# Attention tiles: 512-wide score reductions, transpose copies shared by ScalarE and VectorE, a second P buffer

## The chip, the cores and the metric

One Trainium2 chip, 8 NeuronCores. Each core runs the same program on its own batch element, with no exchange between cores. The metric is the device time in microseconds of the slowest core.

## The reference

Two layers, each an attention whose output is multiplied by a gate made by a feed-forward network, and added to x. Only the attentions matter here:

```python
# layer 0: 16 heads of 128, causal, own K and V per head
scores = jnp.einsum('bhqd,bhkd->bhqk', q, k) * scale
scores = jnp.where(causal, scores, jnp.finfo(scores.dtype).min)
probs = jax.nn.softmax(scores, axis=-1)
attn = jnp.einsum('bhqk,bhkd->bhqd', probs, v)
# layer 1: 16 query heads, one K and one V for all, no mask
scores = jnp.einsum('bhqd,bkd->bhqk', q, k) * SCALE
attn = jax.nn.softmax(scores, axis=-1)
out = jnp.einsum('bhqk,bkd->bhqd', attn, v)
# both layers
x = x + s * g
```

The sequence has 2048 positions, so a head has 16 query tiles of 128 rows.

## The kernel before

The program is a row of phases, each ended on all engines before the next starts: layer norm, QKV, attention, output projection, feed-forward, for each layer, and a final sum. The attention phase (`phase_att`) runs once per layer, with `L` 0 or 1.

A phase is written as one function per engine: `tenf` (TensorE), `vecf` (VectorE), `scaf` (ScalarE), `syncf` (the DMA queue of SyncE). Each engine goes through its own instructions in the written order; nothing is reordered. They meet at semaphores: `bump` gives a point of one engine's work a name, `wt` makes an engine wait for that point. VectorE and ScalarE are moreover fenced (`_Fence`, line 86): each of their instructions waits until the one before on the same engine is complete, so all of them show line 86 in the profile, with small gaps between them.

The loops run over 16 heads `h` and 16 query tiles `qt`. A tile has `nch` score chunks of 512 keys: always 4 in layer 1; in layer 0 1, 2, 3, 4 for tiles 0-3, 4-7, 8-11, 12-15. The first `ha` chunks lie in the PSUM tensor `SCA`, the other `hb` in `SCB`: 1+0, 1+1, 2+1 or 2+2. A tile goes so:

- TensorE multiplies Q and K into `SCA` (L627) once ScalarE's exponential of the last tile has read it, then into `SCB` (L637) likewise.
- VectorE adds the causal mask to the last chunk (layer 0), takes the negated row maximum of `SCA`, then of `SCB` (`TENSOR_REDUCE`), and their minimum, `negm`.
- ScalarE waits for `negm` and for the transposes of the tile before, and writes exp(score + negm) to `PSB` in 16 bits, the row sums to `za` and `zb`: one `ACTIVATE` for `SCA`, one for `SCB`.
- VectorE waits for the last exponential, adds the sums, takes the reciprocal and scales `PSB` in place (mark `pn`).
- TensorE, which has first issued the scores of the tile after, transposes `PSB` in 128x128 blocks (`transp`, L598) into the two halves of the PSUM tensor `PP`, 8 blocks each. Over 8 blocks (three or four chunks) both halves are used.
- ScalarE copies each half to the SBUF tensor `PT` (`ptevac`), after the exponentials of the tile after.

Every four tiles (a group), TensorE multiplies V with `PT` into `OT` (`_att_pv`, L747, 4 to 16 matmuls), once all of the group's copies are done; VectorE copies `OT` out (`CAST P<-OT`). In program order this stands behind the first tile of the next group (tiles 4, 8, 12), and at a head's end behind tile 15. In the text a group boundary is such a tile 4, 8 or 12.

Names in the profile: `P` is the big SBUF tensor, which holds `PSB`, `PT`, Q, K, V and the attention's output; `st` the small statistics tensor.

Of the kernel before, what the change touches and what calls it, by code (L numbers as in the profile page):

```python
# [13 lines left out]
AX = mybir.AxisListType.X  # L14
# [79 lines left out]
class KB:  # L94
# [471 lines left out]
    def phase_att(self, L):  # L566
# [1 line left out]
        causal = (L == 0)  # L568
        QH = [k.Cp[:, 0:2048], k.Cp[:, 2048:4096]]
        VH = [k.Cp[:, 4096:6144], k.Cp[:, 6144:8192]]  # L570
        PSB = k.Cp[:, 8192:10240]
        PT = k.Cp[:, 10240:18432]
        negma = k.st1[:, 0:1]; negmb = k.st1[:, 1:2]; negm = k.st1[:, 2:3]
        za = k.st1[:, 3:4]; zb = k.st1[:, 4:5]; zs = k.st1[:, 5:6]; rz = k.st1[:, 6:7]

        def nchf(qt):
            return qt // 4 + 1 if causal else 4
# [5 lines left out]
        with self.nc.psum_tensor(f"SCA{L}", [128, 1024], F32) as SCA, \  # L583
# [31 lines left out]
            def tenf(t):  # L615
# [3 lines left out]
                for h in range(HEADS):  # L619
                    k.wt(t, f"a{L}qv_{h}")  # L620
                    for qt in range(NT):
                        ha, hb = haf(qt)
                        kbase = h * 2048 if L == 0 else 0
                        if lastA is not None:
                            k.wt(t, lastA)
                        for c in range(ha):
                            ins = t.matmul(SCA[:, c * 512:(c + 1) * 512],  # L627
                                           QH[h % 2][:, qt * 128:(qt + 1) * 128],
                                           k.Bp[:, kbase + c * 512: kbase + c * 512 + 512],
                                           start=True, stop=True)  # L630
                        k.bump(ins, "sT", mark=f"a{L}scA_{h}_{qt}")
                        lastA = f"a{L}expA_{h}_{qt}"
                        if hb:
                            if lastB is not None:
                                k.wt(t, lastB)
                            for c in range(ha, ha + hb):
                                ins = t.matmul(SCB[:, (c - ha) * 512:(c - ha + 1) * 512],  # L637
                                               QH[h % 2][:, qt * 128:(qt + 1) * 128],
                                               k.Bp[:, kbase + c * 512: kbase + c * 512 + 512],
                                               start=True, stop=True)  # L640
                            k.bump(ins, "sT", mark=f"a{L}scB_{h}_{qt}")
                            lastB = f"a{L}expB_{h}_{qt}"
                        if qt > 0:
                            transp(t, h, qt - 1, ppq)
                            if (qt - 1) % 4 == 3:
                                self._att_pv(t, L, h, (qt - 1) // 4, causal, VH, PT, OT)
                    transp(t, h, NT - 1, ppq)
                    self._att_pv(t, L, h, 3, causal, VH, PT, OT)

            def vecf(v):  # L650
                for h in range(HEADS):
                    for qt in range(NT):
                        nch = nchf(qt)
                        ha, hb = haf(qt)
                        off = qt % 4
                        k.wt(v, f"a{L}scA_{h}_{qt}")
                        if causal and hb == 0:
                            v.tensor_tensor(SCA[:, (ha - 1) * 512:ha * 512],
                                            SCA[:, (ha - 1) * 512:ha * 512],
                                            k.msk()[:, off * 512:(off + 1) * 512], OP.add)  # L660
                        ins = v.tensor_reduce(negma, SCA[:, 0:ha * 512], AX, OP.max, negate=True)
                        k.bump(ins, "sV", mark=f"a{L}negA_{h}_{qt}")
                        if hb:
                            k.wt(v, f"a{L}scB_{h}_{qt}")
                            if causal:
                                v.tensor_tensor(SCB[:, (hb - 1) * 512:hb * 512],
                                                SCB[:, (hb - 1) * 512:hb * 512],
                                                k.msk()[:, off * 512:(off + 1) * 512], OP.add)
                            ins = v.tensor_reduce(negmb, SCB[:, 0:hb * 512], AX, OP.max, negate=True)
                            k.bump(ins, "sV", mark=f"a{L}negB_{h}_{qt}")  # L670
                            k.wt(v, f"a{L}negB_{h}_{qt}")
                            ins = v.tensor_tensor(negm, negma, negmb, OP.min)
                        else:
                            k.wt(v, f"a{L}negA_{h}_{qt}")
                            ins = v.tensor_copy(negm, negma)
                        k.bump(ins, "sV", mark=f"a{L}neg_{h}_{qt}")
# [23 lines left out]
            def ptevac(sc, h, qt):  # L700
                nkb = nchf(qt) * 4
                if qt % 4 == 0:
                    if qt > 0:
                        k.wt(sc, f"a{L}pv_{h}_{qt//4 - 1}")
                    elif h > 0:
                        k.wt(sc, f"a{L}pv_{h-1}_3")
                for b in range((nkb + 7) // 8):
                    k.wt(sc, f"a{L}tpb_{h}_{qt}_{b}")
                    j0, j1 = b * 8, min(nkb, b * 8 + 8)
                    dst = PT.rearrange("p (n t) -> p n t", n=16)[:, j0:j1,  # L710
                                                                 (qt % 4) * 128:(qt % 4) * 128 + 128]
                    src = pph[b % 2][:, 0:(j1 - j0) * 128].rearrange("p (n t) -> p n t", n=j1 - j0)
                    ins = sc.copy(dst, src)
                    k.bump(ins, "sS", mark=f"a{L}pte_{h}_{qt}_{b}")
                k.marks[f"a{L}ptall_{h}_{qt}"] = k.marks[f"a{L}pte_{h}_{qt}_{(nkb-1)//8}"]

            def scaf(sc):
                for h in range(HEADS):
                    for qt in range(NT):
                        ha, hb = haf(qt)  # L720
                        k.wt(sc, f"a{L}neg_{h}_{qt}")
                        if qt > 0:
                            k.wt(sc, f"a{L}tp_{h}_{qt-1}")
                        elif h > 0:
                            k.wt(sc, f"a{L}tp_{h-1}_{NT-1}")
                        ins = sc.activation(PSB[:, 0:ha * 512], SCA[:, 0:ha * 512], AF.Exp,
                                            bias=negm, scale=1.0, accum_out=za)
                        k.bump(ins, "sS", mark=f"a{L}expA_{h}_{qt}")
# [610 lines left out]
```

How the kernel before makes its waits and increments, by code:

```python
    def then_inc(self, *a, **kw):  # L52
        return self
# [27 lines left out]
        def f(*args, **kw):  # L81
            kb = self._kb
            sn = self._sname
            kb.sem(sn)
            self._eng.wait_ge(kb.sem_h[sn], kb.cnt.get(sn, 0))
            ins = real(*args, **kw)
            kb.cnt[sn] = kb.cnt.get(sn, 0) + 1
            if not isinstance(ins, _MockIns):
                ins.then_inc(kb.sem_h[sn], 1)
            return ins
# [20 lines left out]
    def bump(self, ins, n, amt=1, mark=None):  # L111
        if n in AUTOMAP:
            sn = AUTOMAP[n]
            self.sem(sn)
            v = self.cnt.get(sn, 0)
            if mark is not None:
                self.marks[mark] = (sn, v)
            return v
        self.sem(n)
        self.cnt[n] += amt
        if mark is not None:
            self.marks[mark] = (n, self.cnt[n])
        if ins is not None and not isinstance(ins, _MockIns):
            ins.then_inc(self.sem_h[n], amt)
        return self.cnt[n]
# [1 line left out]
    def wt(self, eng, mark):  # L127
        got = self.marks.get(mark)
        if got is None:
            if self.mock:
                return
            raise KeyError(f"unresolved mark {mark}")
        n, v = got
        eng.wait_ge(self.sem(n), v)
# [1 line left out]
    def wtv(self, eng, n, v):  # L136
        eng.wait_ge(self.sem(n), v)
# [166 lines left out]
            def syncf(sy):  # L304
# [14 lines left out]
                    if L == 1:  # L319
                        k.wt(sy, f"ln{L}x1_{i}")
                        sy.dma_start(out=k.x1_h[i], in_=XF[i % 2][:]).then_inc(k.sem("st"), 16)
                        k.bump(None, "st", 16)
```

## Time and profile before

| | us |
|---|---|
| runs of the kernel | 12421.89 and 12107.16, median 12264.52 |
| the profiled execution | 12111.88 |
| its span on the slowest core (5) | 12110.3 |
| spans of the 8 cores | 12086.5 to 12110.3 |
| busy: TensorE, VectorE, ScalarE | 7344.6, 3957.8, 2841.2 |
| attention of layer 0, of layer 1 (first score matmul to the next stage's first rows) | 2042, 2425 |

The profile is of one execution. Its views used below are the busy time of each engine in a stretch, the timeline (each instruction with its start, its length, how long its engine was idle before it and who released it), and groups of like instructions with their mean length. PE is TensorE, PEld its weight loads, DVE VectorE, ACT ScalarE. The granted clock is a share of 2.4 GHz.

### The profile page before, as it was taken

What the parts mean: (1) busy time and instruction counts of PE and PEld (TensorE: products, weight loads), DVE (VectorE), ACT (ScalarE), POOL (GpSimd) and SP (SyncE); (2) the same over time, 40 slices, a digit from 0 to 9 for tenths busy, and PEclk for the clock granted to TensorE, in tenths of its full rate; (3) what the DMA queues carried; (4) which work ended last, traced back from release to release, by engine and by line L of the source; (5) the groups of instructions that cost most, each with busy time, mean ns of one, the idle gap of its engine ahead of it and who ended that gap; (6) DMA issues with size and microseconds to landing.
All of it is one profiled execution on the core that took longest, in us unless ns stands there. A gap on an engine that the chain in (4) does not pass through costs nothing. (4 is left out here: it accounts for less than half of the span.)

```text
span 12110.3 us, 107998 instructions; the slowest of 8 cores (12086.5 to 12110.3 us)
## 1 busy us (share of the span) xinstructions
PE 7344.6 (61%) x35408; PEld 3415.2 (28%) x35408; DVE 3957.8 (33%) x6488; ACT 2841.2 (23%) x4586; POOL 134.9 (1%) x233
## 2 busy tenths in 40 slices
PE   1299444444379999183650855555554799997791
PEld 0144211111134444031220322222222344443340
DVE  4421344444314444815312244444443111110002
ACT  2200333333301111212112044444444000000000
POOL 0000000000000000000000000000000000000000
PEclk9999655555689999596775955555555899998995
DMA  1233000000132331132233300000000322223444
GB/s 47 51 61 56 21 11 7 11 7 11 28 89 48 61 61 37 40 70 49 55 99 130 73 8 8 7 8 7 8 8 13 85 47 53 53 53 81 108 79 168
DMA packets 426199, 581.07 MB, mean 48 GB/s; under 512 B 257200, under 2 KB 347312, under 8 KB 401456
## 3 DMA queue, kind: packets, MB, share of 16 engines
q0 software_dynamic: 75216, 237.39, 11.9%
q1 hardware_dynamic: 350432, 336.77, 8.9%
q8 instruction: 293, 4.80, 0.2%
q14 instruction: 258, 2.11, 0.1%
HBM read 655.71 MB, written 155.71 MB: 67 GB/s over the span
## 5 line engine op out<-in xcount | busy, mean ns | idle before, releaser
L86 DVE TENSOR_TENSOR P<-P 128x512 f32<-128x512 f32 (+6 forms) x700 | 691.5, 988 | 1674.5 <-DMA P<-g_hb 1603.1
L627 PE MATMUL SCA<-P 128*128 128x512 bf16 x896 | 410.7, 540 | 1175.8 <-ACT P L86 1148.6
L86 ACT ACTIVATE P<-SCA,st 128x1024 bf16<-128x1024 f32 (+1 forms) x512 | 516.9, 1010 | 2318.5 <-DVE st L86 2318.5
L598 PE MATMUL PP<-identS,P 128*128 128x128 bf16 x6656 | 731.5, 292 | 473.5 <-DVE P L86 451.0
L747 PE MATMUL OT<-P 128*128 128x512 bf16 x1664 | 619.9, 550 | 622.1 <-ACT P L86 622.1
L488 PE MATMUL QP<-P 128*128 128x512 bf16 x4224 | 919.3, 380 | 24.4 <-DMA P<-wqk 12.9
L86 ACT COPY P<-PP 128x1024 bf16<-128x1024 bf16 (+1 forms) x896 | 853.2, 952 | 105.9 <-PE PP L598 26.3
L598 PEld LDWEIGHTS PP<-identS,P 128*128 128x128 bf16 x6656 | 625.4, 134 | 793.7 <-issue 776.7
L1126 PE MATMUL F1G<-P 128*128 128x512 bf16 x2816 | 622.3, 382 | 176.3 <-DVE P L86 116.9
L1216 PE MATMUL F1D<-P 128*128 128x512 bf16 x2816 | 618.8, 381 | 118.5 <-SPq L1181 118.5
L860 PE MATMUL F0P<-P 128*128 128x512 bf16 x2816 | 638.6, 380 | 70.2 <-DMA P<-w 70.2
L864 PE MATMUL F0P<-P 128*128 128x512 bf16 x2816 | 636.5, 379 | 0.0
L1039 PE MATMUL F0D<-P 128*128 128x512 bf16 x2816 | 617.2, 381 | 3.4 <-ACT P L86 3.4
L1132 PE MATMUL F1U<-P 128*128 128x512 bf16 x2816 | 615.0, 379 | 0.0
L86 DVE TENSOR_TENSOR st<-st 128x1 f32<-128x1 f32 x928 | 147.6, 159 | 1334.5 <-ACT P L86 1216.6
L86 DVE TENSOR_REDUCE st<-SCA 128x1 f32<-128x1024 f32 (+1 forms) x512 | 558.7, 1091 | 70.4 <-PE SCA L627 16.4
L488 PEld LDWEIGHTS QP<-P 128*128 128x128 bf16 x4224 | 413.5, 98 | 523.1 <-issue 31.4
L774 PE MATMUL WOP<-P 128*128 128x512 bf16 x2048 | 445.8, 381 | 109.1 <-POOLq L763 109.1
L437 PE MATMUL TP<-identS,P 128*128 128x128 bf16 x512 | 59.7, 308 | 741.5 <-ACT P L86 741.5
L86 DVE TENSOR_REDUCE st<-SCB 128x1 f32<-128x1024 f32 (+1 forms) x448 | 480.5, 1072 | 49.0 <-DVE SCB L86 3.7
L86 DVE TENSOR_SCALAR P<-F1U,us_s 128x2048 f32<-128x2048 f32 x44 | 103.4, 2351 | 1200.4 <-PE F1U L1132 1200.4
L747 PEld LDWEIGHTS OT<-P 128*128 128x128 bf16 x1664 | 206.0, 129 | 992.6 <-issue 955.5
(85 smaller groups left out, 6429.8 us busy)
## 6 DMA issues: line engine op xcount, KB each, us to landing
P<-w POOLq DMA_DIRECT2D x22, 2048.0 KB, 30.6
P<-w2p POOLq DMA_DIRECT2D x32, 1408.0 KB, 11.7
P<-wgu POOLq DMA_DIRECT2D x44, 1024.0 KB, 9.3
P<-wd POOLq DMA_DIRECT2D x32, 1408.0 KB, 10.5
P<-x SPq DMA_DIRECT2D x32, 1024.0 KB, 5.2
gn_hb<-P SPq DMA_DIRECT2D x176, 128.0 KB, 1.7
P<-gn_hb SPq DMA_DIRECT2D x176, 128.0 KB, 2.1
hf_h<-P SPq DMA_DIRECT2D x44, 512.0 KB, 5.9
```

Source lines behind the costliest of these rows:

```text
L86: ins = real(*args, **kw)
L488: ins = t.matmul(pq, WS[n % 2][:, ht * 128:(ht + 1) * 128], k.A[:, ht * 2048 + tc * 512: ht * 2048 + tc * 512 + 512], start=(ht == 0), sto ...
L598: ins = t.transpose(pph[half][:, (j - j0) * 128:(j - j0 + 1) * 128], PSB[:, j * 128:(j + 1) * 128], k.ident[:])
L627: ins = t.matmul(SCA[:, c * 512:(c + 1) * 512], QH[h % 2][:, qt * 128:(qt + 1) * 128], k.Bp[:, kbase + c * 512: kbase + c * 512 + 512], st ...
L747: ins = t.matmul(OT[:], VH[h % 2][:, kt * 128:(kt + 1) * 128], PT[:, kt * 512:(kt + 1) * 512], start=(kt == 0), stop=(kt == ktn - 1))
L774: ins = t.matmul(pq, k.A[:, hd * 2048 + ts * 128: hd * 2048 + ts * 128 + 128], k.Bp[:, hd * 2048 + ec * 512: hd * 2048 + ec * 512 + 512], ...
L860: t.matmul(X1[pp], k.Bp[:, ht * 2048 + tt * 128: ht * 2048 + tt * 128 + 128], W1S[fc % 2][:, ht * 512:(ht + 1) * 512], start=(ht == 0), st ...
L864: ins = t.matmul(X3[pp], k.Bp[:, ht * 2048 + tt * 128: ht * 2048 + tt * 128 + 128], W3S[fc % 2][:, ht * 512:(ht + 1) * 512], start=(ht == ...
L1039: ins = t.matmul(DN[:, half * 1024 + tc * 512: half * 1024 + tc * 512 + 512], W2L[nn % 2][:, ft * 128:(ft + 1) * 128], iq2[ft][:, tc * 512 ...
L1126: t.matmul(GP[:, tc * 512:(tc + 1) * 512], WG[ft % 4][:, ht * 128:(ht + 1) * 128], k.Bp[:, ht * 2048 + tc * 512: ht * 2048 + tc * 512 + 51 ...
L1132: ins = t.matmul(UP[:, tc * 512:(tc + 1) * 512], WU[ft % 4][:, ht * 128:(ht + 1) * 128], k.Bp[:, ht * 2048 + tc * 512: ht * 2048 + tc * 51 ...
L1216: ins = t.matmul(DN[:, half * 1024 + tc * 512: half * 1024 + tc * 512 + 512], WD[nn % 2][:, ft * 128:(ft + 1) * 128], hfm[ft][:, tc * 512: ...
```

## The change

Four edits in the attention phase.

1. Reductions by chunk. TensorE marks each score chunk, and VectorE reduces each chunk of 512 by itself, into `ngp[c]`, then takes the minimum of two to four values in one to three instructions.
2. The second half of a tile's transposes (blocks 8 to 15) is copied to `PT` by VectorE, the first half by ScalarE as before. VectorE does it behind the scaling of the tile after, and PV waits for every copy's own mark.
3. In layer 1 `PSB` has two buffers; the exponential waits for the transposes of two tiles back. In layer 0 both names are the one buffer.
4. The statistics move to other columns of `st1` and `st2`.

```diff
-        PSB = k.Cp[:, 8192:10240]
+        PSBs = ([k.Cp[:, 8192:10240], k.Cp[:, 18432:20480]] if L == 1
+                else [k.Cp[:, 8192:10240], k.Cp[:, 8192:10240]])
...
                         for c in range(ha):
-                            ins = t.matmul(SCA[:, c * 512:(c + 1) * 512],
+                            ins = t.matmul(scslice(c, qt),
...
-                        k.bump(ins, "sT", mark=f"a{L}scA_{h}_{qt}")
+                            k.bump(ins, "sT", mark=f"a{L}scc_{h}_{qt}_{c}")
...
+                        for c in range(nch):
+                            k.wt(v, f"a{L}scc_{h}_{qt}_{c}")
+                            sl = scslice(c, qt)
+                            if causal and c == nch - 1:
+                                v.tensor_tensor(sl, sl, k.msk()[:, off * 512:(off + 1) * 512], OP.add)
+                            ins = v.tensor_reduce(ngp[c], sl, AX, OP.max, negate=True)
+                        k.bump(ins, "sV")
+                        k.wtv(v, "sVa", k.cnt["sVa"])
+                        if nch == 1:
+                            ins = v.tensor_copy(negm, ngp[0])
+                        elif nch == 2:
+                            ins = v.tensor_tensor(negm, ngp[0], ngp[1], OP.min)
+                        elif nch == 3:
+                            v.tensor_tensor(tmp, ngp[0], ngp[1], OP.min)
+                            ins = v.tensor_tensor(negm, tmp, ngp[2], OP.min)
+                        else:
+                            v.tensor_tensor(tmp, ngp[0], ngp[1], OP.min)
+                            v.tensor_tensor(negm, ngp[2], ngp[3], OP.min)
+                            ins = v.tensor_tensor(negm, negm, tmp, OP.min)
+                        k.bump(ins, "sV", mark=f"a{L}neg_{h}_{qt}")
                         ha, hb = haf(qt)
-                        k.wt(v, f"a{L}scA_{h}_{qt}")
...
-                        ins = v.tensor_reduce(negma, SCA[:, 0:ha * 512], AX, OP.max, negate=True)
...
-                            ins = v.tensor_reduce(negmb, SCB[:, 0:hb * 512], AX, OP.max, negate=True)
...
-                            ins = v.tensor_tensor(negm, negma, negmb, OP.min)
...
+                        PSB = PSBs[qt % 2]
                         ins = v.tensor_scalar_mul(PSB[:, 0:nch * 512], PSB[:, 0:nch * 512], rz)
                         k.bump(ins, "sV", mark=f"a{L}pn_{h}_{qt}")
+                        if qt > 0:
+                            self._ptevac_v(v, L, h, qt - 1, nchf, pph, PT)
...
+                    self._ptevac_v(v, L, h, NT - 1, nchf, pph, PT)
                     k.wt(v, f"a{L}pv_{h}_3")
...
+                        if L == 0:
+                            if qt > 0:
+                                k.wt(sc, f"a{L}tp_{h}_{qt-1}")
...
+                            if qt > 1:
+                                k.wt(sc, f"a{L}tp_{h}_{qt-2}")
...
+    def _ptevac_common(self, eng, semn, L, h, qt, nchf, pph, PT, parity):
...
+        for b in range(nb):
+            if b % 2 != parity:
+                continue
...
+            k.wt(eng, f"a{L}tpb_{h}_{qt}_{b}")
...
+            if semn == "sS":
+                ins = eng.copy(dst, src)
+            else:
+                ins = eng.tensor_copy(dst, src)
...
+    def _ptevac_s(self, sc, L, h, qt, nchf, pph, PT):
+        self._ptevac_common(sc, "sS", L, h, qt, nchf, pph, PT, parity=0)
...
+    def _ptevac_v(self, v, L, h, qt, nchf, pph, PT):
+        self._ptevac_common(v, "sV", L, h, qt, nchf, pph, PT, parity=1)
...
-        k.wt(t, f"a{L}ptall_{h}_{4*g+3}")
+        for qq in range(4 * g, 4 * g + 4):
+            nkb = ((qq // 4 + 1) if causal else 4) * 4
+            for b in range((nkb + 7) // 8):
+                k.wt(t, f"a{L}pte_{h}_{qq}_{b}")
```

VectorE's row at a group boundary and the tile behind it, layer 1, before. `sT`, `sSa` and `sVa` are the semaphores of TensorE, ScalarE and VectorE:

```order
L86 TENSOR_SCALAR P<-P,st 128x2048 [waits sVa]
L86 CAST P<-OT 128x512 [waits sT,sVa]
L86 TENSOR_REDUCE st<-SCA 128x1 [waits sT,sVa]
L86 TENSOR_REDUCE st<-SCB 128x1 [waits sT,sVa]
L86 TENSOR_TENSOR st<-st 128x1 [waits sVa]
L86 TENSOR_TENSOR st<-st 128x1 [waits sSa,sVa]
L86 RECIPROCAL st<-st 128x1 [waits sVa]
L86 TENSOR_SCALAR P<-P,st 128x2048 [waits sVa]
L86 TENSOR_REDUCE st<-SCA 128x1 [waits sT,sVa]
```

The same place in the changed kernel (`x2`, `x3`: so many alike in a row):

```order
L86 TENSOR_SCALAR P<-P,st 128x2048 [waits sVa]
L86 COPY P<-PP 128x8x128 [waits sT,sVa]
L86 CAST P<-OT 128x512 [waits sT,sVa]
L86 TENSOR_REDUCE st<-SCA 128x1 [waits sT,sVa] x2
L86 TENSOR_REDUCE st<-SCB 128x1 [waits sT,sVa] x2
L86 TENSOR_TENSOR st<-st 128x1 [waits sVa] x3
L86 TENSOR_TENSOR st<-st 128x1 [waits sSa,sVa]
L86 RECIPROCAL st<-st 128x1 [waits sVa]
L86 TENSOR_SCALAR P<-P,st 128x2048 [waits sVa]
L86 COPY P<-PP 128x8x128 [waits sT,sVa]
L86 TENSOR_REDUCE st<-SCA 128x1 [waits sT,sVa] x2
```

The copy stands between the scaling and whatever follows it, `OT`'s read or the next tile's reductions; there are four reductions for two and three minima for one. The `TENSOR_TENSOR` that waits for `sSa` is the sum of `za` and `zb`.

ScalarE's row over two inner tiles of layer 1, before:

```order
L86 COPY P<-PP 128x8x128 [waits sT,sSa] x2
L86 ACTIVATE P,st<-SCA,st 128x1024 [waits sVa,sT,sSa]
L86 ACTIVATE P,st<-SCB,st 128x1024 [waits sSa]
L86 COPY P<-PP 128x8x128 [waits sT,sSa] x2
L86 ACTIVATE P,st<-SCA,st 128x1024 [waits sVa,sT,sSa]
```

and in the changed kernel:

```order
L86 COPY P<-PP 128x8x128 [waits sT,sSa]
L86 ACTIVATE P,st<-SCA,st 128x1024 [waits sVa,sT,sSa]
L86 ACTIVATE P,st<-SCB,st 128x1024 [waits sSa]
L86 COPY P<-PP 128x8x128 [waits sT,sSa]
L86 ACTIVATE P,st<-SCA,st 128x1024 [waits sVa,sT,sSa]
```

One of the two copies per tile is gone; the rest stands where it stood.

## Rows read from the trace of the kernel before

**Rows 1.** Stretches of both attention stages: busy us (xinstructions) by engine, TensorE's granted clock.
```profile
1271.00:3313.00 2042.00, 825.70 (x3840) 378.64 (x3840) 899.82 (x1792) 767.47 (x1281) 8.46 (x16) 0.58 0.06 12
6936.00:9361.00 2425.00, 1234.46 (x6163) 589.80 (x6160) 988.15 (x1601) 1141.49 (x1540) 1.78 (x4) 0.59 0.03 8
```

**Rows 2.** Timeline, an inner layer-1 tile: start us, us, engine, instruction [idle before <-releaser].
```profile
8061.29 1.12 ACT L86 ACTIVATE P<-SCA,st 128x1024 bf16<-128x1024 f32 x1 [2.59 <-DVE st L86]
...
8063.89 2.11 ACT L86 COPY P<-PP 128x1024 bf16<-128x1024 bf16 x2
...
8063.97 0.16 DVE L86 TENSOR_TENSOR st<-st 128x1 f32<-128x1 f32 x1 [2.88 <-ACT P L86]
...
8064.64 0.75 DVE L86 TENSOR_SCALAR P<-P,st 128x2048 bf16<-128x2048 bf16 x1 [0.17 <-DVE st L86]
8065.50 1.23 DVE L86 TENSOR_REDUCE st<-SCA 128x1 f32<-128x1024 f32 x1
...
8065.65 1.87 PE L598 MATMUL PP<-identS,P 128*128 128x128 bf16 x16 [0.69 <-DVE P L86]
8066.83 1.23 DVE L86 TENSOR_REDUCE st<-SCB 128x1 f32<-128x1024 f32 x1
8068.23 0.16 DVE L86 TENSOR_TENSOR st<-st 128x1 f32<-128x1 f32 x1 [0.17 <-DVE st L86]
8068.59 1.12 ACT L86 ACTIVATE P<-SCA,st 128x1024 bf16<-128x1024 f32 x1 [2.59 <-DVE st L86]
```

**Rows 3.** VectorE's groups by form: out<-in shapes xcount | busy us, mean ns | idle.
```profile
L86 DVE TENSOR_REDUCE st<-SCA 128x1 f32<-128x1024 f32 x384 | 470.2, 1224 | 57.2 <-PE SCA L627 16.4 <-DVE P L86 2.4
...
L86 DVE TENSOR_REDUCE st<-SCA 128x1 f32<-128x512 f32 x128 | 88.5, 692 | 13.2
...
L86 DVE CAST PI<-P 128x512 int32<-128x512 f32 x176 | 75.2, 427 | 18.2
...
L86 DVE TENSOR_SCALAR P<-P,st 128x1024 bf16<-128x1024 bf16 x64 | 31.1, 486 | 11.2 <-DVE st L86 11.2
...
L86 DVE TENSOR_SCALAR P<-P,st 128x512 bf16<-128x512 bf16 x64 | 22.6, 353 | 11.2 <-DVE st L86 11.2
L86 DVE CAST PI<-P 128x1024 int32<-128x1024 f32 x32 | 22.2, 694 | 3.3
```

**Rows 4.** Timeline, a group boundary of layer 1.
```profile
7214.76 2.11 ACT L86 COPY P<-PP 128x1024 bf16<-128x1024 bf16 x2
...
7215.52 0.75 DVE L86 TENSOR_SCALAR P<-P,st 128x2048 bf16<-128x2048 bf16 x1 [0.18 <-DVE st L86]
...
7217.12 6.22 PE L747 MATMUL OT<-P 128*128 128x512 bf16 x16 [6.03 <-ACT P L86]
...
7223.52 0.69 DVE L86 CAST P<-OT 128x512 bf16<-128x512 f32 x1 [7.25 <-PE OT L747]
7223.61 0.59 PE L637 MATMUL SCB<-P 128*128 128x512 bf16 x2
...
7227.40 1.12 ACT L86 ACTIVATE P<-SCA,st 128x1024 bf16<-128x1024 f32 x1 [10.52 <-DVE st L86]
```

**Rows 5.** Timeline, layer 0, tile 12 of a head.
```profile
3093.67 1.69 ACT L86 COPY P<-PP 128x1024 bf16<-128x1024 bf16 x2
...
3095.61 4.47 PE L747 MATMUL OT<-P 128*128 128x512 bf16 x12 [6.84 <-ACT P L86]
```

**Rows 6.** Timeline, a head's end in layer 1.
```profile
8146.46 0.75 DVE L86 TENSOR_SCALAR P<-P,st 128x2048 bf16<-128x2048 bf16 x1 [0.18 <-DVE st L86]
...
8151.02 5.20 PE L747 MATMUL OT<-P 128*128 128x512 bf16 x16 [1.69 <-ACT P L86]
```

**Rows 7.** Timeline, two weight loads early in a PV.
```profile
7180.44 0.15 PEld L747 LDWEIGHTS OT<-P 128*128 128x128 bf16 x1 [0.28 <-issue]
7180.87 0.15 PEld L747 LDWEIGHTS OT<-P 128*128 128x128 bf16 x1 [0.28 <-issue]
```

**Rows 8.** The page's group of PV matmuls: xcount | busy us, mean ns | idle.
```profile
L747 PE MATMUL OT<-P 128*128 128x512 bf16 x1664 | 619.9, 550 | 622.1 <-ACT P L86 622.1
```

More of the change, by code:

```diff
@@ L570, in phase_att @@
         VH = [k.Cp[:, 4096:6144], k.Cp[:, 6144:8192]]
-        PSB = k.Cp[:, 8192:10240]
+        PSBs = ([k.Cp[:, 8192:10240], k.Cp[:, 18432:20480]] if L == 1
+                else [k.Cp[:, 8192:10240], k.Cp[:, 8192:10240]])
         PT = k.Cp[:, 10240:18432]
-        negma = k.st1[:, 0:1]; negmb = k.st1[:, 1:2]; negm = k.st1[:, 2:3]
-        za = k.st1[:, 3:4]; zb = k.st1[:, 4:5]; zs = k.st1[:, 5:6]; rz = k.st1[:, 6:7]
+        ngp = [k.st2[:, j:j + 1] for j in range(4)]
+        negm = k.st1[:, 0:1]; za = k.st1[:, 1:2]; zb = k.st1[:, 2:3]
+        zs = k.st1[:, 3:4]; rz = k.st1[:, 4:5]; tmp = k.st1[:, 5:6]
         def nchf(qt):
@@ L587, in phase_att, with scslice @@
             pph = [PP[:, 0:1024], PP[:, 1024:2048]]
+            def scslice(c, qt):
+                ha, hb = haf(qt)
+                if c < ha:
+                    return SCA[:, c * 512:(c + 1) * 512]
+                return SCB[:, (c - ha) * 512:(c - ha + 1) * 512]
             def transp(t, h, qt, ppq):
                 nkb = nchf(qt) * 4
+                PSB = PSBs[qt % 2]
                 k.wt(t, f"a{L}pn_{h}_{qt}")
@@ L636, in tenf @@
                             for c in range(ha, ha + hb):
-                                ins = t.matmul(SCB[:, (c - ha) * 512:(c - ha + 1) * 512],
+                                ins = t.matmul(scslice(c, qt),
                                                QH[h % 2][:, qt * 128:(qt + 1) * 128],
@@ L640, in tenf @@
                                                start=True, stop=True)
-                            k.bump(ins, "sT", mark=f"a{L}scB_{h}_{qt}")
+                                k.bump(ins, "sT", mark=f"a{L}scc_{h}_{qt}_{c}")
                             lastB = f"a{L}expB_{h}_{qt}"
@@ L653, in vecf @@
                         nch = nchf(qt)
-                        ha, hb = haf(qt)
-                        off = qt % 4
-                        k.wt(v, f"a{L}scA_{h}_{qt}")
[L657 to L660, printed above, removed]
-                        ins = v.tensor_reduce(negma, SCA[:, 0:ha * 512], AX, OP.max, negate=True)
@@ L662, in vecf @@
[L662 to L668, printed above, removed]
-                            ins = v.tensor_reduce(negmb, SCB[:, 0:hb * 512], AX, OP.max, negate=True)
-                            k.bump(ins, "sV", mark=f"a{L}negB_{h}_{qt}")
-                            k.wt(v, f"a{L}negB_{h}_{qt}")
-                            ins = v.tensor_tensor(negm, negma, negmb, OP.min)
-                        else:
-                            k.wt(v, f"a{L}negA_{h}_{qt}")
-                            ins = v.tensor_copy(negm, negma)
@@ L676, in vecf @@
-                        k.bump(ins, "sV", mark=f"a{L}neg_{h}_{qt}")
+                        off = qt % 4
+                        for c in range(nch):
[4 more added lines that the diff above has]
+                            ins = v.tensor_reduce(ngp[c], sl, AX, OP.max, negate=True)
@@ L687, in vecf @@
                         k.wt(v, f"a{L}rz_{h}_{qt}")
+                        PSB = PSBs[qt % 2]
                         ins = v.tensor_scalar_mul(PSB[:, 0:nch * 512], PSB[:, 0:nch * 512], rz)
                         k.bump(ins, "sV", mark=f"a{L}pn_{h}_{qt}")
+                        if qt > 0:
+                            self._ptevac_v(v, L, h, qt - 1, nchf, pph, PT)
                         if qt % 4 == 0 and qt >= 4:
@@ L698, in vecf @@
                     k.marks[f"a{L}hdone_{h}"] = k.marks[f"a{L}oev_{h}_3"]
[L700 to L715, printed above, removed]
             def scaf(sc):
@@ L720, in scaf @@
                         ha, hb = haf(qt)
+                        PSB = PSBs[qt % 2]
                         k.wt(sc, f"a{L}neg_{h}_{qt}")
[L722 to L725, printed above, removed]
+                        if L == 0:
+                            if qt > 0:
+                                k.wt(sc, f"a{L}tp_{h}_{qt-1}")
+                            elif h > 0:
+                                k.wt(sc, f"a{L}tp_{h-1}_{NT-1}")
+                        else:
+                            if qt > 1:
+                                k.wt(sc, f"a{L}tp_{h}_{qt-2}")
+                            elif h > 0:
+                                k.wt(sc, f"a{L}tp_{h-1}_{NT-2+qt}")
                         ins = sc.activation(PSB[:, 0:ha * 512], SCA[:, 0:ha * 512], AF.Exp,
@@ L734, in scaf @@
                         if qt > 0:
-                            ptevac(sc, h, qt - 1)
-                    ptevac(sc, h, NT - 1)
+                            self._ptevac_s(sc, L, h, qt - 1, nchf, pph, PT)
+                    self._ptevac_s(sc, L, h, NT - 1, nchf, pph, PT)
             self.phase(f"att{L}", {"tensor": tenf, "vector": vecf, "scalar": scaf, "sync": syncf})
+    def _ptevac_common(self, eng, semn, L, h, qt, nchf, pph, PT, parity):
+        k = self
+        nkb = nchf(qt) * 4
+        nb = (nkb + 7) // 8
+        for b in range(nb):
+            if b % 2 != parity:
+                continue
+            if qt % 4 == 0:
+                if qt > 0:
+                    k.wt(eng, f"a{L}pv_{h}_{qt//4 - 1}")
+                elif h > 0:
+                    k.wt(eng, f"a{L}pv_{h-1}_3")
+            k.wt(eng, f"a{L}tpb_{h}_{qt}_{b}")
+            j0, j1 = b * 8, min(nkb, b * 8 + 8)
+            dst = PT.rearrange("p (n t) -> p n t", n=16)[:, j0:j1,
+                                                         (qt % 4) * 128:(qt % 4) * 128 + 128]
+            src = pph[b % 2][:, 0:(j1 - j0) * 128].rearrange("p (n t) -> p n t", n=j1 - j0)
+            if semn == "sS":
+                ins = eng.copy(dst, src)
+            else:
+                ins = eng.tensor_copy(dst, src)
+            k.bump(ins, semn, mark=f"a{L}pte_{h}_{qt}_{b}")
+    def _ptevac_s(self, sc, L, h, qt, nchf, pph, PT):
+        self._ptevac_common(sc, "sS", L, h, qt, nchf, pph, PT, parity=0)
+    def _ptevac_v(self, v, L, h, qt, nchf, pph, PT):
+        self._ptevac_common(v, "sV", L, h, qt, nchf, pph, PT, parity=1)
     def _att_pv(self, t, L, h, g, causal, VH, PT, OT):
```

## The prediction

> **What bounds the kernel now.** First the busy time of each engine by stage [rows 1]. The two attention stages, which alone the diff touches, take 2042 us (layer 0) and 2425 us (layer 1) of the 12110 us span. No engine is full in them: in layer 1 TensorE is busy 1234 us, ScalarE 1141 us, VectorE 988 us. A stage in which three engines are each about half busy is a chain that hands work round, so the next view is the timeline of one inner tile of layer 1 [rows 2]. There the first exponential starts at 8061.29 and the next tile's at 8068.59: a pitch of 7.30 us. In between, VectorE waits 2.88 us for the second exponential, then runs its rows with no gap over 0.18 us: sum of the two partial sums, reciprocal, scaling of P (ends 8065.39), two score reductions, minimum, and ScalarE starts 0.20 us later. So VectorE's work after the exponentials and ScalarE's two exponentials take turns. ScalarE's two transpose copies (2.11 us from 8063.89) lie beside VectorE's turn and end at 8066.00, 2.6 us before ScalarE is wanted again. TensorE's scores and transposes lie beside it too.
>
> There is one exception, once in four tiles: PV needs all the copied transposes, and VectorE then needs PV and the next scores. In [rows 4] the copies end at 7216.87, PV starts at 7217.12, VectorE's read of OT starts at 7223.52 and the next exponential at 7227.40. At a head's end it is the same with the last transposes in front [rows 6].
>
> **What the change does to VectorE's turn.** VectorE gets three kinds of work, all in its turn, none in its wait. A gap between two fenced VectorE instructions is 0.10 us (8065.50 plus 1.23 to 8066.83 [rows 2]).
> - Reductions. A 1024-wide one takes 1.225 us, a 512-wide one 0.692 [rows 3]; the halves pay the fixed part twice. Four chunks: 4 x 0.692 + 3 x 0.10 = 3.07 against 2 x 1.225 + 0.10 = 2.55, so +0.52 us. Three chunks: 2 x 0.692 + 0.10 - 1.225 = +0.26. One or two chunks: the same instructions as before.
> - Minima. One per tile becomes three with four chunks, two with three. Each added one costs 0.16 [rows 2] and a gap of 0.10: +0.52 and +0.26.
> - So a four-chunk tile gains 1.04 us and a three-chunk tile 0.52. Layer 1 has 256 of the first, layer 0 has 64 of each: 320 x 1.04 + 64 x 0.52 = **366 us**.
> - Copies. Where a tile has over eight key blocks, its second copy moves from ScalarE to VectorE, behind the next tile's scaling of P. The kernel before has no VectorE copy of 16-bit data out of PSUM, so the duration (E) is bounded. From above: VectorE's cast of 32-bit data out of PSUM (OT) takes 0.69 us for 512 elements [rows 4], like the PSUM reduction with 0.692, whose 1024 take 1.225; at that rate E is 1.225 for 1024 and 0.692 for 512. From below: 16-bit data inside SBUF at 0.486 and 0.353 [rows 3]. Between them: a 32-bit cast inside SBUF takes 0.427 for 512 and 0.694 for 1024, 0.52 ns per added element, the reductions out of PSUM 1.04 ns, the 16-bit SBUF scaling 0.26 ns. So PSUM halves the rate and 16-bit data double it; both together give 0.52 ns per element, and with the fixed 0.16 us E is 0.69 for 1024 and 0.42 for 512. I take that.
>
> Where the copy lies on the path, it costs E + 0.10. That is the case at the inner tiles with a previous tile to copy: 11 per head in layer 1 and 2 in layer 0 with 1024 elements (208 in all, 0.79 each, 164 us), and 3 per head in layer 0 with 512 (48, 0.52 each, 25 us). **189 us.** A head's first tile copies nothing.
>
> **The group boundaries.** With e the end of the second exponential, put 0.09 us before ScalarE's copies start, PV started at e + 2.45 in layer 1 (7217.12 against 7214.67 [rows 4]). Now VectorE's copy is last: P's scaling ends at e + 1.60 (7215.52 + 0.75), the copy starts at e + 1.70, and PV 0.25 us after it ends: e + 1.95 + E. That is E - 0.50, or +0.19 us, 48 times. In layer 0 at tile 12 PV started at e + 2.02 [rows 5]; now e + 1.95 + 0.42, +0.35 us, 16 times. At a head's end [rows 6] PV starts 3.81 us after P's scaling ends (8147.21 to 8151.02). Now ScalarE copies one half while TensorE transposes the other: transposes start at +0.26 and last 1.86, as in [rows 2], so they end at +2.12, VectorE's copy runs from +2.3 to +3.0, PV starts at +3.3, so -0.5 us, 32 times. The three together: 9 + 6 - 16 = **-1 us**. PV, OT's read and the next scores are unchanged.
>
> **Edits at nothing.** The second P buffer of layer 1 lets the exponential start before the previous transposes are done; but those end at 8067.51, 1.1 us before the next exponential [rows 2], and P's next scaling and reductions come in VectorE's own order, so it frees nothing. The marks per score chunk let a reduction start a chunk earlier, but in [rows 4] the last scores end at 7224.20, with OT's read (7224.21), and at an inner tile they are done well before VectorE's turn. ScalarE sheds 1.01 us per tile that was beside VectorE's turn. On TensorE only waits change: the second half's transposes of a tile wait for VectorE's copy of the tile before, queued right behind P's scaling; they end some 2 us after the scaling, against reductions and minima of over 4 us. Behind them on TensorE stands, at a boundary, PV, which waits for more anyway.
>
> **Sum.** 366 + 189 - 1 = 554 us. The profiled execution took 12111.9 us, 1.6 over its span, so 12666 us, +4.6%. The median of the two runs shown, 12264.5, is 153 above it (12107.2 and 12421.9); on that base it would be 12818. Some 2% is what a measurement here tells from no change.
>
> **Rivals.**
> 1. VectorE copies 16-bit data out of PSUM no faster than it casts OT [rows 4]. Copies: 208 x 1.325 + 48 x 0.79 = 314; boundaries 48 x 0.73 + 16 x 0.62 = 45; at a head's end the transposes wait for the first copy and the last ends late, +0.4, 32 times, 13. Sum 366 + 372 = 738: **12850 us**. For it: every VectorE read of PSUM in the trace goes so. Against: all those data are 32-bit.
> 2. It copies at the SBUF rate: 208 x 0.586 + 48 x 0.453 = 144; boundaries 3; head ends 32 x -0.75 = -24. Sum 489: **12601 us**. Against: casts from PSUM are slower than in SBUF.
> 3. The clock. TensorE is granted 0.58 and 0.59 in these stages [rows 1], a mix of its levels 1.2 and 2.4 GHz. PV starts at the lower one, with a load every 0.43 us [rows 7], and ends at the higher. Longer tiles make TensorE idle more. If every PV stayed low, 1664 matmuls x 0.43 = 716 us against 620 now [rows 8]: +96 on top of the forecast, **12762 us**. Against: PV comes after about 6 us without TensorE work already, and its own length is what lifts the clock. No gain is to be had here, since nothing makes TensorE busier.
> 4. The other side: the added work falls into VectorE's wait. Per inner tile of layer 1 that is 1.04 + 0.79 = 1.83 us, and VectorE is idle 2.88 us before each z sum [rows 2]. If it fits there, only the boundaries' -1 remains: **12111 us**, no change. It decides at one point: whether one reduction of the next tile, or the copy, stands ahead of the wait for the exponentials. In the order of the changed kernel all of them stand behind the z sum, reciprocal and scaling, and the minimum feeding ScalarE stands behind them. That they should pass it is near excluded.
>
> **How the numbers follow.** Forecast 0.70; rival 1 0.15; rival 2 0.05; rival 3 0.06; rival 4 0.03, and 0.01 for something that makes it faster. Slower by over 2% is the forecast and rivals 1 to 3: 0.96. Within 2%: 0.03. Faster: 0.01. The range reaches from a little under rival 2, 12560, to rival 1 with the clock's 96 on top, 12946, so 12960, which also holds the forecast on the median's base. The likeliest case's own range, gaps of 0.10 to 0.17 taken, is 12630 to 12760.
>
> **What would show it.** In the changed profile: a VectorE group P<-PP at 0.69 us for 1024 elements (1.23 or 0.49 for rivals 1, 2); 512-wide reductions of 0.69 in fours; the inner pitch of layer 1 at 7.30 + 1.83 = 9.1 us; VectorE's wait of 2.88 us unchanged before each z sum (gone under rival 4); stages longer by about 406 us (layer 1) and 148 us (layer 0); PV 0.2 us later after the exponential; other stages unchanged. Inner pitches near 7.3 would make the prediction wrong at its root.

## The result, and the profile after

The changed kernel's profiled execution took 12674.3 us against 12111.9 before: +562.4. The measured ratio is 1.0452, with a 95% interval of 1.0388 to 1.0517: slower. The forecast, 12666 us or 1.0458, is 8 us from that execution. Yet the median of the 11 runs of the changed kernel is 12967.1 us, 7 us above the range, and that of the kernel before rose from 12264.5 us (2 runs) to 12496.4 (10 runs). In most runs of either kernel the cores of one die, sometimes of both, have a lower granted clock than in the two profiled executions and take longer, so the ratio above and every span below are of runs or dies for which that is not so.

The stages, to set beside [rows 1]. The window begins and ends with the attention; columns as there:

```profile
1271.00:3459.00 2188.00, 803.57 (x3768) 381.09 (x3840) 1032.01 (x2304) 663.85 (x1153) 8.46 (x16) 0.57 0.06 12
7094.00:9921.00 2827.00, 1219.22 (x6056) 594.97 (x6160) 1326.72 (x2881) 880.80 (x1284) 0.00 (x0) 0.58 0.03 7
```

Layer 0's attention is now 2188 us long where it was 2042, layer 1's 2827 where the same measure (last cast of `QP` to last cast of `OT`) gives 2421. VectorE is busy 339 us more in layer 1 and ScalarE 261 us less. The granted clock is 0.57 and 0.58 where it was 0.58 and 0.59. The ends of the stages come from these rows of the operations on `SCA`, `WOP`, `QP` and `OT` (duration min/median/max in ns, first and last start in us):

```profile
L636 PEld LDWEIGHTS SCA<-P x896: 95/105/152, 1271.7 to 9900.7; 128*128 128x128 bf16 x180
...
L808 PEld LDWEIGHTS WOP<-P x2048: 97/98/152, 3459.3 to 10195.7; 128*128 128x128 bf16 x187
...
L86 DVE CAST P<-QP x136: 690/692/693, 785.0 to 7094.1; 128x512 bf16<-128x512 f32 x136
...
L86 DVE CAST P<-OT x128: 690/692/692, 1297.7 to 9921.0; 128x512 bf16<-128x512 f32 x128
```

One inner tile of layer 1, timeline (start us, length us, engine, instruction, idle before it), answers to [rows 2]:

```profile
9722.14 1.11 ACT L86 ACTIVATE P<-SCA,st 128x1024 bf16<-128x1024 f32 x1 [5.53 <-DVE st L86]
...
9724.73 1.01 ACT L86 COPY P<-PP 128x1024 bf16<-128x1024 bf16 x1
...
9724.82 0.16 DVE L86 TENSOR_TENSOR st<-st 128x1 f32<-128x1 f32 x1 [2.88 <-ACT P L86]
...
9725.49 0.75 DVE L86 TENSOR_SCALAR P<-P,st 128x2048 bf16<-128x2048 bf16 x1 [0.18 <-DVE st L86]
9726.34 0.69 DVE L86 COPY P<-PP 128x1024 bf16<-128x1024 bf16 x1
...
9726.49 1.86 PE L607 MATMUL PP<-identS,P 128*128 128x128 bf16 x16 [0.69 <-DVE P L86]
9727.14 1.49 DVE L86 TENSOR_REDUCE st<-SCA 128x1 f32<-128x512 f32 x2
9728.72 1.49 DVE L86 TENSOR_REDUCE st<-SCB 128x1 f32<-128x512 f32 x2
9730.38 0.69 DVE L86 TENSOR_TENSOR st<-st 128x1 f32<-128x1 f32 x3 [0.17 <-DVE st L86]
9731.27 1.11 ACT L86 ACTIVATE P<-SCA,st 128x1024 bf16<-128x1024 f32 x1 [5.53 <-DVE st L86]
```

The pitch is 9731.27 - 9722.14 = 9.13 us (it was 7.30). The wait ahead of the sum of `za` and `zb` is 2.88 us as before: nothing added went into it. Behind the scaling stand the copy (0.69), two pairs of reductions (1.49 each) and three minima (0.69 with their gaps). ScalarE's copy ends at 9725.74 and the transposes at 9728.35, both well ahead of the exponential at 9731.27; so neither is on the path.

VectorE's groups by form, beside [rows 3]:

```profile
L86 DVE TENSOR_REDUCE st<-SCA 128x1 f32<-128x512 f32 x896 | 619.6, 692 | 109.0 <-PE SCA L636 15.8 <-DVE P L86 0.6 <-PE PP L607 0.5
...
L86 DVE COPY P<-PP 128x1024 bf16<-128x1024 bf16 x320 | 221.3, 692 | 77.6 <-PE PP L607 47.9
...
L86 DVE COPY P<-PP 128x512 bf16<-128x512 bf16 x64 | 27.2, 425 | 6.6
```

The copy of 16-bit data out of PSUM takes 692 ns for 1024 elements and 425 ns for 512.

A group boundary of layer 1, beside [rows 4]. The record of PV's first matmul is missing, so its weight load (PEld) is shown:

```profile
9699.12 1.01 ACT L86 COPY P<-PP 128x1024 bf16<-128x1024 bf16 x1
...
9699.87 0.75 DVE L86 TENSOR_SCALAR P<-P,st 128x2048 bf16<-128x2048 bf16 x1 [0.17 <-DVE st L86]
9700.73 0.69 DVE L86 COPY P<-PP 128x1024 bf16<-128x1024 bf16 x1
9701.64 0.14 PEld L781 LDWEIGHTS OT<-P 128*128 128x128 bf16 x2 [8.26 <-issue]
...
9708.08 0.69 DVE L86 CAST P<-OT 128x512 bf16<-128x512 f32 x1 [6.67 <-PE OT L781]
...
9713.01 1.11 ACT L86 ACTIVATE P<-SCA,st 128x1024 bf16<-128x1024 f32 x1 [12.88 <-DVE st L86]
```

With e = 9699.03 (0.09 before ScalarE's copy starts), PV's first load is at e + 2.61. Its matmul is put 0.03 later, at e + 2.64, as at the head's end below, where both rows are there. From `OT`'s read to the next exponential it is 4.93 us, where [rows 4] has 3.88.

A head's end, beside [rows 6]:

```profile
9734.62 0.75 DVE L86 TENSOR_SCALAR P<-P,st 128x2048 bf16<-128x2048 bf16 x1 [0.18 <-DVE st L86]
...
9735.62 1.86 PE L607 MATMUL PP<-identS,P 128*128 128x128 bf16 x16 [7.27 <-DVE P L86]
9736.78 1.01 ACT L86 COPY P<-PP 128x1024 bf16<-128x1024 bf16 x1 [1.90 <-PE PP L607]
9737.66 0.69 DVE L86 COPY P<-PP 128x1024 bf16<-128x1024 bf16 x1 [1.50 <-PE PP L607]
...
9738.57 0.14 PEld L781 LDWEIGHTS OT<-P 128*128 128x128 bf16 x2 [1.36 <-issue]
9738.60 1.01 PE L781 MATMUL OT<-P 128*128 128x512 bf16 x2 [1.12 <-DVE P L86]
```

From the end of the scaling (9735.37) to PV's first load it is 3.20 us and to its first matmul, 0.03 later, 3.23, where it was 3.81. VectorE's copy at 9737.66 is the last thing PV waits for. The PV matmuls themselves, beside [rows 8] (64 of their 1664 records are missing):

```profile
L781 PE MATMUL OT<-P 128*128 128x512 bf16 x1600 | 609.1, 555 | 751.4 <-DVE P L86 572.9
```

That is 381 ns for each recorded one against 373.

### The profile page after: what moved, and what is told of

Its sections match the earlier page's. It is cut to its first block and busy times, and to the rows that moved or that the text cites. A ratio compares the mean times of both kernels' runs of the same rounds, so it can differ in the third digit from the quotient of the medians.

```text
span 12672.8 us, 111725 instructions; the slowest of 8 cores (12645.2 to 12672.8 us)
## 1 busy us (share of the span) xinstructions
PE 7284.8 (57%) x34753; PEld 3424.2 (27%) x35408; DVE 4428.6 (35%) x8280; ACT 2475.0 (20%) x4202; POOL 135.0 (1%) x233
## 5 line engine op out<-in xcount | busy, mean ns | idle before, releaser
L636 PE MATMUL SCA<-P 128*128 128x512 bf16 x792 | 383.4, 557 | 1555.3 <-ACT P L86 1541.5
L86 DVE TENSOR_TENSOR st<-st 128x1 f32<-128x1 f32 x1632 | 259.4, 159 | 1404.3 <-ACT P L86 1214.0
L86 DVE TENSOR_REDUCE st<-SCA 128x1 f32<-128x512 f32 x896 | 619.6, 692 | 109.0 <-PE SCA L636 15.8
L86 DVE TENSOR_REDUCE st<-SCB 128x1 f32<-128x512 f32 x768 | 531.1, 691 | 80.1 <-DVE st L86 0.9
L636 PEld LDWEIGHTS SCA<-P 128*128 128x128 bf16 x896 | 73.7, 105 | 1673.6 <-issue 1654.0
L86 ACT COPY P<-PP 128x1024 bf16<-128x1024 bf16 (+1 forms) x512 | 490.9, 959 | 104.9 <-PE PP L607 61.9
```

What stands on the lines that cost most here:

```text
L86: ins = real(*args, **kw)
L636: ins = t.matmul(scslice(c, qt), QH[h % 2][:, qt * 128:(qt + 1) * 128], k.Bp[:, kbase + c * 512: kbase + c * 512 + 512], start=True, stop= ...
```

## The experiments

The lengths of the two attention stages serve as the measure. Over the eight cores of a profiled execution they differ by some 16 us at most, and mostly by under 10, also where the spans differ by hundreds. Each length below is the median of the eight cores; the table at the end of this section has their range. Every difference is between such medians.

**Reductions undone.** VectorE reduces `SCA` and `SCB` whole again and takes one minimum.

```diff
-                        for c in range(nch):
-                            k.wt(v, f"a{L}scc_{h}_{qt}_{c}")
...
-                            ins = v.tensor_reduce(ngp[c], sl, AX, OP.max, negate=True)
+                        k.wt(v, f"a{L}scc_{h}_{qt}_{ha-1}")
...
+                        ins = v.tensor_reduce(ngp[0], SCA[:, 0:ha * 512], AX, OP.max, negate=True)
...
+                            ins = v.tensor_reduce(ngp[1], SCB[:, 0:hb * 512], AX, OP.max, negate=True)
```

> The changed kernel with its reductions undone: VectorE reduces SCA and SCB whole (1024 wide with four chunks) and takes one minimum per tile; copies and buffers stay changed. Theory (VectorE's turn is on the path in full): 366 us come back, 266 in layer 1 and 100 in layer 0, so about 12308 us, and the inner pitch of layer 1 goes from 9.13 to 8.09 us. Rival (the loss is TensorE's lower clock or the longer waits for copies, and the marks per chunk gain something): undoing the reductions gives back under 100 us, the pitch stays above 8.7.

Measured: layer 1 took 2565 us, 264 less than with the change, layer 0 2077, 109 less; the span was 12273 to 12299 us. Timeline of an inner tile of layer 1 in this run:

```profile
8003.78 1.11 ACT L86 ACTIVATE P<-SCA,st 128x1024 bf16<-128x1024 f32 x1 [4.48 <-DVE st L86]
...
8007.98 0.69 DVE L86 COPY P<-PP 128x1024 bf16<-128x1024 bf16 x1
...
8008.77 1.23 DVE L86 TENSOR_REDUCE st<-SCA 128x1 f32<-128x1024 f32 x1
8010.10 1.22 DVE L86 TENSOR_REDUCE st<-SCB 128x1 f32<-128x1024 f32 x1
...
8011.86 1.11 ACT L86 ACTIVATE P<-SCA,st 128x1024 bf16<-128x1024 f32 x1 [4.48 <-DVE st L86]
```

The pitch is 8.08 us, 1.05 less than 9.13, as the theory has it. The rival, under 100 us, falls.

**Copies back on ScalarE.**

```diff
-            if b % 2 != parity:
+            if parity == 1:
                 continue
```

> The changed kernel with both transpose copies on ScalarE again; reductions and buffers stay changed. Theory: the 189 us of copies at inner tiles come back and the boundaries' -1 too, about 12486 us, inner pitch of layer 1 8.34 us. Rival (sharing the copies relieves ScalarE, which is busy beside it): the time does not fall, or rises, since ScalarE gets 1.01 us per tile more.

Measured: layer 1 2692 us, 137 less than with the change; layer 0 2136, 50 less. The spans, on one die each of two runs, were 12454 to 12465 and 12452 to 12487 us. The inner pitch of layer 1 is 8.33 us. The time fell, so the sharing did not relieve anything that mattered.

**One P buffer.**

```diff
-        PSBs = ([k.Cp[:, 8192:10240], k.Cp[:, 18432:20480]] if L == 1
+        PSBs = ([k.Cp[:, 8192:10240], k.Cp[:, 8192:10240]] if L == 1
...
-                        if L == 0:
+                        if True:
                             if qt > 0:
                                 k.wt(sc, f"a{L}tp_{h}_{qt-1}")
```

> The changed kernel with one P buffer in layer 1 as before. Theory: the second buffer frees nothing, so no change, 12674 us within 10. Rival (it lets exponentials start earlier, which hid part of the loss): slower by over 50 us.

Measured: layer 1 2831 us (2829 with two buffers), span 12639 to 12662. No change. The second buffer bought nothing in this order. One of the nine executions of this kernel took 24904 us, on all cores far longer than any other; nothing on record says why, and it is not used here.

**VectorE's copy ahead of its wait.** The same instruction, one place earlier in VectorE's order: behind the minimum, before the sum of `za` and `zb`.

```diff
                         k.bump(ins, "sV", mark=f"a{L}neg_{h}_{qt}")
+                        if qt > 0:
+                            self._ptevac_v(v, L, h, qt - 1, nchf, pph, PT)
                         ha, hb = haf(qt)
...
-                        if qt > 0:
-                            self._ptevac_v(v, L, h, qt - 1, nchf, pph, PT)
```

> The changed kernel with VectorE's copy moved from behind the scaling of P to ahead of the wait for the exponentials, so that it falls into the 2.88 us in which VectorE waits. Theory (place in VectorE's order decides, not the work): the 189 us of inner tiles go, and at group boundaries PV no longer waits for VectorE but for ScalarE's one copy, 1.3 us earlier in layer 1 (48 times) and 1.0 in layer 0 (16 times): -189 -62 -16 = -267, about 12407 us, inner pitch 8.34 us. Rival (the copy costs wherever it stands, for instance because VectorE and ScalarE disturb each other when both read PSUM): the exponentials get longer than 1.11 us and the time falls by less than 100 us.

Measured: 12413 us in the run in which all cores had a granted clock of 0.765 to 0.767; layer 1 2636 us (-193), layer 0 2130 (-57), together -250 where -267 was expected. Timeline in layer 1, an inner tile and then a boundary:

```profile
8033.17 0.69 DVE L86 COPY P<-PP 128x1024 bf16<-128x1024 bf16 x1
8033.28 1.11 ACT L86 ACTIVATE P<-SCA,st 128x1024 bf16<-128x1024 f32 x1 [4.74 <-DVE st L86]
...
8035.95 0.16 DVE L86 TENSOR_TENSOR st<-st 128x1 f32<-128x1 f32 x1 [2.08 <-ACT P L86]
...
8041.61 1.11 ACT L86 ACTIVATE P<-SCA,st 128x1024 bf16<-128x1024 f32 x1 [4.73 <-DVE st L86]
...
8052.54 1.01 ACT L86 COPY P<-PP 128x1024 bf16<-128x1024 bf16 x1
...
8053.91 6.23 PE L781 MATMUL OT<-P 128*128 128x512 bf16 x16 [6.05 <-ACT P L86]
```

The copy now runs under the exponential, whose 1.11 us it leaves alone: VectorE reading `PP` does not slow ScalarE reading `SCA`. The wait ahead of the sum shrank from 2.88 to 2.08 us, by just the copy and its gap, and the pitch is 8.33 us. At the boundary PV starts at 8053.91, 1.46 us after e (8052.45), 0.11 later than expected. So the copy's cost was its place. Rival 4 described a working mechanism; only the written order kept the change from it.

**First and fourth together.** What stays of the change costs VectorE's turn nothing. The diff is the sum of both.

> The first and fourth experiment together: whole reductions and one minimum as in the kernel before, VectorE's copy inside its wait for the exponentials. What is left of the change is the part that costs VectorE's turn nothing. Theory: the inner pitch of layer 1 is 7.30 us as before; PV starts 1.1 us earlier than before at 48 boundaries of layer 1 and 0.7 at 16 of layer 0, and 0.5 earlier at 32 head ends: -53 -11 -16 = -80, about 12032 us, under 1%. Rival (parts interact, the sum of single parts does not hold): above 12100 us.

Measured: layer 1 2366 us and layer 0 2023, that is 55 and 16 less than before, 71 where 80 was expected; one run took 12042.3 us, two of the kernel before on the same chip 12132.2 and 12134.1. The inner pitch of layer 1 is 7.29 us. It is the change without its cost, and worth 0.7%, less than the 2% that a measurement here tells from no change; the stage lengths show it.

**First and second together.** Only the marks per chunk, PV's waits on single copies and the second buffer stay.

> The first and second experiment together: whole reductions, one minimum, both copies on ScalarE. Of the change only the marks per chunk, PV's waits for single copies and the second P buffer of layer 1 are left. Theory: these cost and give nothing, so both attention stages are as long as before, 2040 and 2421 us within 5. Rival (a part of the loss comes from TensorE's more numerous marks and waits): over 20 us longer together.

Measured: 2039 us and 2422 us, 1 us more than before each, span 12082 to 12100. Marks and waits are free here, and the two parts undone carry the whole loss.

**The other order.** VectorE does the reductions and minimum of the next tile first, and the sum, reciprocal and scaling of the last tile behind them, where ScalarE is at its exponentials. TensorE transposes two tiles back. This needs a second set of `negm`, `za`, `zb` and three P buffers, which lie in parts of the big SBUF tensor that attention leaves free (in layer 0 the output columns of heads not yet computed, later the keys of finished heads). Reductions are whole. In outline:

```diff
+                for n in range(NN + 3):
+                    if n < NN:
...
+                        ins = v.tensor_tensor(negm, ngp[0], ngp[1], OP.min)
...
+                    if 1 <= n < NN + 1:
+                        h1, q1 = divmod(n - 1, NT)
...
+                        ins = v.tensor_scalar_mul(PSB[:, 0:nch * 512], PSB[:, 0:nch * 512], rz)
...
+                    if 2 <= n < NN + 2:
+                        h2, q2 = divmod(n - 2, NT)
+                        self._ptevac_v(v, L, h2, q2, nchf, pph, PT)
```

> The other side of rival 4 made real: the z sum, reciprocal and scaling of a tile stand behind the reductions and minimum of the next tile on VectorE, the transposes come two tiles after the scores on TensorE, VectorE's copy two tiles later, with three P buffers and two sets of negm, za, zb; reductions whole, one minimum. Theory (the order on VectorE is the bound): the scaling (1.4 us) and the copy run beside ScalarE's exponentials and the first reduction beside the second exponential; the cycle is second exponential's end, scores into SCB, second reduction, minimum, exponential: about 5.5 us in place of 7.30 in layer 1, and PV lies partly beside VectorE and ScalarE; layer 1 about 1630 us in place of 2421, layer 0 some 350 less than 2042, so about 10970 us. Rival (TensorE in its written order becomes the bound, since scores now stand behind transposes and PV that wait for copies): pitch over 6.5 us and less than 500 us gained.

Measured: layer 1 1666 us, layer 0 1508, span 10785 to 10831 us against 12048 to 12133 for the kernel before on the same chip: 10.6% less. Layer 1 is 36 us from its forecast; layer 0 lost 530 us where some 350 were forecast, and why it lost more was not sought. The medians over all runs, 11512 (8 runs) and 12582 (11 runs), have a ratio of 0.915. Timeline in layer 1:

```profile
6606.94 1.11 ACT L86 ACTIVATE P<-SCA,st 128x1024 bf16<-128x1024 f32 x1 [2.02 <-PE PP L619]
...
6607.51 0.75 DVE L86 TENSOR_SCALAR P<-P,st 128x2048 bf16<-128x2048 bf16 x1 [0.18 <-DVE st L86]
...
6608.29 1.01 PE L651 MATMUL SCA<-P 128*128 128x512 bf16 x2 [1.36 <-ACT P L86]
6608.36 0.69 DVE L86 COPY P<-PP 128x1024 bf16<-128x1024 bf16 x1
...
6609.48 1.22 DVE L86 TENSOR_REDUCE st<-SCA 128x1 f32<-128x1024 f32 x1 [0.42 <-PE SCA L651]
...
6609.59 1.01 PE L661 MATMUL SCB<-P 128*128 128x512 bf16 x2 [0.29 <-ACT P L86]
...
6610.69 1.86 PE L619 MATMUL PP<-identS,P 128*128 128x128 bf16 x16
6610.80 1.23 DVE L86 TENSOR_REDUCE st<-SCB 128x1 f32<-128x1024 f32 x1
6612.20 0.42 DVE L86 TENSOR_TENSOR st<-st 128x1 f32<-128x1 f32 x2 [0.17 <-DVE st L86]
6612.56 1.11 ACT L86 ACTIVATE P<-SCA,st 128x1024 bf16<-128x1024 f32 x1 [2.02 <-PE PP L619]
...
6617.86 3.62 PE L799 MATMUL OT<-P 128*128 128x512 bf16 x16
...
6621.31 0.59 PE L651 MATMUL SCA<-P 128*128 128x512 bf16 x2
```

The pitch is 6612.56 - 6606.94 = 5.62 us. The scaling (6607.51) and the copy (6608.36) run under the exponentials. After that VectorE waits 0.42 us for scores instead. Two paths now end within 0.02 us of each other: the scores into `SCA`, issued behind the first exponential, are reduced until 6610.70, and the scores into `SCB`, issued behind the second, are done at 6610.60; the second reduction starts at 6610.80. The last exponential's row names the transposes (they end at 6612.55) as its releaser, but they are of another P buffer than the one it writes; by the program it waits for the minimum, the first of the two at 6612.20, and starts 0.20 us after it. At inner tiles TensorE waits for ScalarE (1.36 us before the scores at 6608.29) and not the other way round, so the rival, a pitch above 6.5 us set by TensorE's order, falls there. At a boundary PV (6617.86) takes 3.6 us and the scores (6621.31) wait behind it, as the rival has it. Part of the gain is the clock's: the granted clock of layer 1 is 0.71 where it was 0.59, and the PV matmuls of both layers are busy 483.7 us in all where [rows 8] has 619.9. No run separates this from the gain by the order itself.

| kernel | layer 0, us | layer 1, us | spans, us | expected, us |
|---|---|---|---|---|
| before | 2034 to 2042 | 2420 to 2421 | 12086 to 12110 | |
| changed | 2183 to 2188 | 2820 to 2830 | 12645 to 12673 | 12666 |
| reductions undone | 2074 to 2080 | 2564 to 2575 | 12273 to 12299 | 12308 |
| copies on ScalarE | 2131 to 2141 | 2692 to 2696 | 12452 to 12487 | 12486 |
| one P buffer | 2185 to 2187 | 2826 to 2836 | 12639 to 12662 | 12674 |
| copy ahead of the wait | 2127 to 2132 | 2635 to 2638 | 12369 to 12412 | 12407 |
| first and fourth | 2020 to 2023 | 2363 to 2368 | 12008 to 12041 | 12032 |
| first and second | 2035 to 2044 | 2421 to 2426 | 12082 to 12100 | as before |
| other order | 1501 to 1518 | 1666 to 1671 | 10785 to 10831 | 10970 |

## Why the prediction was right in its steps and wrong in its range

- *What bounds the kernel.* Right. VectorE's turn and ScalarE's exponentials alternate; the experiment that moved one copy into the wait, and the one that reordered the turn, show it.
- *Reductions and minima, 366 us.* Put at 266 and 100. Measured with the copies in place 264 and 109; with the copies on ScalarE 270 and 97.
- *Copies, 189 us with the boundaries' -1.* Put at 140 for layer 1 and 48 for layer 0. Measured with the new reductions in place 137 and 50; with the whole reductions 143 and 38. Parts measured singly and together differ by up to 12 us in layer 0, where the masks and the tiles' sizes vary; what makes up those 12 us was not sought.
- *E = 0.69 and 0.42.* Measured 0.692 and 0.425. Scaling the rate of 32-bit data out of PSUM by the gain that 16-bit data have inside SBUF gave the right value; rivals 1 and 2 fall. The trace agrees with what the Trainium skill ("VectorE: DVE Perf Modes", section "Walkthrough: the 8-slice pipeline in each mode") says of PSUM's one read port and of packed 16-bit reads.
- *Boundaries and head ends.* PV at e + 2.64, forecast e + 1.95 + E = 2.64. Head's end 3.20 to 3.23 us, forecast 3.3.
- *Edits at nothing.* Right: one buffer, and marks without the rest, change nothing.
- *Rival 3, the clock.* Granted clock down by 0.01 in both stages, the PV matmuls longer by about 8 ns each, 13 us over 1664: nothing like 96. The stages came out 408 and 148 us longer, against 406 and 148.
- *Sum.* 554 forecast, 562 measured between the two profiled executions and 556 in the two stages. Outside them, core by core, the time changed by -11 to +27 us.

**The step that failed is the base under the range, and with it the upper end.** "The range reaches from a little under rival 2, 12560, to rival 1 with the clock's 96 on top, 12946, so 12960". Every bound in it was added to the profiled execution's 12112 us. The term for how far a median lies above that execution was put at nothing for rival 1 and for the clock; only the likeliest case got it, at 153 us, which gave 12818. It measured 384 us for the kernel before (12496 against 12112, ten runs) and 293 for the changed kernel (12967 against 12674, eleven runs from 12672 to 13712). So 12112 + 554 + 384 would have been 13050, 83 above the measured median; 12112 + 562 + 293 is that median. Two runs 315 us apart could not tell where a median of ten lies, but they did show that the spread is as wide as the terms in dispute. That the miss is only 7 us is chance: the bound at 12960 was built from a slower copy and a lower clock, and neither came. Mechanism, terms and difference were right; the number to be hit was a median, and the spread of its base was no term of the range.

Where that spread lies is seen between the cores of one execution, the profiled one of the kernel with the reductions undone. Cores 0 and 7 spanned 12276 and 12645 us. Ahead of layer 0's attention they took 1264 and 1341 us, in it 2074 and 2080, in the stages between the attentions 3629 and 3919, and in layer 1's attention 2564 and 2567. The attention stages, in which TensorE waits most of the time, hardly differ; the 370 us lie in the stages around them, which the diff leaves alone. So the changed part of this kernel says little of the range of the median; the spread of its runs does. What makes the spread is open.

## What to carry to other kernels

Where two engines take turns, ask of each added instruction whether it stands in its engine's turn or in its wait; the total idle time of the engine says nothing of that. The same copy cost 0.79 us per tile behind the scaling and nothing ahead of the wait. Reordering such a turn so that the next tile's critical part comes before the last tile's leftovers gave more (10.6%) than the best division of the work tried here (0.7%). A second P buffer alone gave nothing; the reordered kernel was built with three, and fewer were not tried with it. And a range for a median needs the spread between executions as a term of its own, laid on every bound, not on the centre alone.

## What the runs showed of the hardware

- VectorE copied 16-bit data from PSUM to SBUF at 0.52 ns per element (692 and 425 ns for 1024 and 512), into runs of 128 elements, while ScalarE read another PSUM tensor: the exponential stayed at 1.11 us. The rate was forecast; that the two engines leave each other alone was the point in doubt. ScalarE took 1.01 us for the same 1024 elements.
- A fenced VectorE instruction costs 0.10 to 0.18 us of gap however small it is: the three minima of a tile, 0.16 us each, start 0.17 us after the reduction and take 0.69 us in a row.
